# The value's causal convolution as products with diagonal tap matrices

## The reference, cut to what matters

```python
def _short_conv(x, w):
    K = w.shape[-1]                                  # 4
    xp = jnp.pad(x, ((0, 0), (K - 1, 0), (0, 0)))
    y = jnp.zeros_like(x)
    for k in range(K):
        y = y + xp[:, k:k + L, :] * w[:, k]
    return y
...
q = x @ Wq.T;  k = x @ Wk.T;  v = x @ Wv.T
beta = sigmoid(x @ Wb.T)
q = silu(_short_conv(q, conv_q)); k = silu(_short_conv(k, conv_k)); v = silu(_short_conv(v, conv_v))
q = l2norm(q);  k = l2norm(k)                        # per head of 16 channels
# delta rule, per head and token: v_new = (v - k S) * beta;  S += k v_new;  o = q S
```

## Time and profile before

| what | us |
|---|---|
| median of 3 runs (lowest to highest) | 3052.33 (3044.51 to 3056.43) |
| the profiled execution's own time | 3045.67 |
| its span, first to last instruction | 3043.5 |
| VectorE busy in the span | 2124.9 (70%) |
| TensorE products busy in the span | 2498.7 (82%) |
| TensorE weight loads busy | 1887.2 (62%) |
| ScalarE busy in the span | 1605.3 (53%) |
| mean granted TensorE clock | 0.875 |

### The profile page before, as it was taken

How to read it: one execution, slowest core, us unless ns; L and a number is a source line. 1 busy time by engine, 2 the same in 40 slices (tenths; PEclk the granted TensorE clock), 3 DMA queues, 4 the chain that set the end, 5 groups by cost and what they waited for, 6 DMA issues and landing times. The chain is left out here.

```text
span 3043.5 us, 109358 instructions
## 1 busy us (share of the span) xinstructions
PE 2498.7 (82%) x45968; PEld 1887.2 (62%) x45968; DVE 2124.9 (70%) x5160; ACT 1605.3 (53%) x2896; POOL 1112.7 (37%) x1092
## 2 busy tenths in 40 slices
PE   4578887788888878788778999999978898987665
PEld 2345555556565555555566888888867676765443
DVE  4878988899889999888835222222325676878996
ACT  5454555555465554455124555555546666665442
POOL 0000233333333333233433777777744333332000
PEclk8778888888888898788679999999999899999877
DMA  2000122122222122113235999998798575754431
GB/s 66 8 11 10 49 74 71 53 79 75 71 74 73 55 79 73 63 69 111 84 114 172 301 310 305 306 305 296 258 336 305 202 275 209 268 217 173 161 107 28
DMA packets 191579, 448.61 MB, mean 147 GB/s; under 512 B 34034, under 2 KB 83700, under 8 KB 182772
## 3 DMA queue, kind: packets, MB, share of 16 engines
q1 hardware_dynamic: 129652, 284.26, 28.5%
q0 software_dynamic: 52224, 148.97, 12.9%
q10 hardware_dynamic: 9216, 8.39, 0.9%
HBM read 266.07 MB, written 175.42 MB: 145 GB/s over the span
## 5 line engine op out<-in xcount | busy, mean ns | idle before, releaser
L1041 POOL DMA_INDIRECT scr_xs<-xn_r,idx x512 | 534.1, 1043 | 1136.8 <-PE ps L473 479.7
L1068 POOL DMA_INDIRECT scr_ys<-y,idx_t x576 | 578.4, 1004 | 548.0 <-ACT sg L1333 253.1
L712 PE MATMUL ps<-xT,wr 128*128 128x256 f32 (+1 forms) x2560 | 563.5, 364 | 4.7 <-DVE h L2053 4.7
L2053 DVE TENSOR_TENSOR h<-sg,ps 128x256 f32<-128x256 f32 x320 | 125.2, 393 | 532.8 <-ACT sg L1333 532.2
L712 PEld LDWEIGHTS ps<-xT,wr 128*128 128x128 f32 x2560 | 439.1, 193 | 56.1 <-issue 14.1
L720 PE MATMUL ps<-wr,h 128*128 128x256 f32 x1152 | 312.3, 390 | 56.4 <-ACT y L1340 56.3
L1340 ACT ACTIVATE y<-ps,of_row 128x256 f32<-128x256 f32 x576 | 244.8, 471 | 145.2 <-PE ps L720 139.8
L720 PEld LDWEIGHTS ps<-wr,h 128*128 128x128 f32 x1152 | 218.5, 195 | 89.3 <-issue 62.1
L1680 DVE TENSOR_TENSOR tu<-tu,tmp 128x60 f32<-128x60 f32 (+14 forms) x480 | 242.5, 505 | 16.5
L527 PE MATMUL ps<-sq,w_proj 128*128 128x512 f32 x512 | 249.7, 624 | 5.1 <-issue 2.4
L1677 DVE TENSOR_TENSOR tmp<-tu 128x60 f32<-128x60 f32 (+14 forms) x480 | 241.6, 503 | 13.4
(11 more groups left out here) (268 smaller groups left out, 4231.6 us busy)
## 6 DMA issues: line engine op xcount, KB each, us to landing
wr<-in_wexp SPq DMA_DIRECT2D x224, 384.0 KB, 4.5
xt<-scr_xs SPq DMA_DIRECT2D x256, 280.0 KB, 4.2
yg<-scr_ys SPq DMA_DIRECT2D x64, 1024.0 KB, 7.4
scr_ys<-y,idx_t POOLq DMA_INDIRECT x576
scr_xs<-zeros SPq DMA_DIRECT2D x64, 140.0 KB
xt<-scr_xs SPq DMA_DIRECT2D x64, 140.0 KB
x_in<-in_x SPq DMA_DIRECT2D x64, 128.0 KB, 3.1
x_res<-in_x SPq DMA_DIRECT2D x64, 128.0 KB, 2.6
```

The source lines that it names most:

```text
L712: last = pe.matmul(ps[:, bank, half * TILE:half * TILE + wide], wr[:, w % NW, at:at + EI], xT2[:, t % NH, k, 0:wide], start=k == 0, stop=k ...
L1041: nc.gpsimd.indirect_dma_start(xs[int(i >= FIRST)][:, :], bass.IndirectOffsetOnAxis(idx[:, i % NR, c, k:k + 1], 0), xn_r[:, i % NR, c, :], ...
L1068: nc.gpsimd.indirect_dma_start(ys[int(t >= NTH[0])][:, :], bass.IndirectOffsetOnAxis(idx_t[:, t % NRT, r:r + 1], 0), y2[:, t % NY, r, :], ...
```

## The change: what it does, and the diff

The value tiles (4 and 5) are convolved on TensorE. At the start VectorE multiplies the identity by each tap's column and so makes eight diagonal 128x128 matrices. `value_taps` accumulates four products in a PSUM bank, one a tap, with the shifted `raw` as the moving operand; `value_silus` takes the silu straight from that bank. ScalarE no longer makes the scaled copy of the value tiles, and VectorE no longer runs their taps. Queries and keys stay as they were. Two small constants are placed and loaded later, to make room. A new semaphore, `s_values`, tells VectorE that the values are there; `s_silu` and `s_conv` count four tiles a block where they counted six.

```diff
...
+        v_taps = sb1("v_taps", [P, G, KC, P])
...
+            def value_taps(i, g):
+                n = 2 * G + g
+                bank = into(f"TAP{n}", i)
+                ring.emptied(pe, f"PROJ{n}", i)
+                for k in range(KC):
+                    last = pe.matmul(ps[:, bank, :].rearrange("p (b t) -> p b t", b=B), v_taps[:, g, k, :],
+                                     raw[:, n, :, k:k + TB], start=k == 0, stop=k == KC - 1)
+                done(last, bank)
...
                 if A:
+                    value_taps(a, 1)
                     project(a, 7)
                     project(a, 4)
...
                 if A:
+                    value_taps(a, 0)
                     norms(a, 0)
...
-                    nc.scalar.activation(conv[:, n, :].rearrange("p (b c t) -> p b c t", b=B, c=NC), by_chunk,
-                                         ACT.Copy, scale=conv_w[:, n // G, n % G, HIST:])
+                    if n < 2 * G:
+                        nc.scalar.activation(conv[:, n, :].rearrange("p (b c t) -> p b c t", b=B, c=NC), by_chunk,
+                                             ACT.Copy, scale=conv_w[:, n // G, n % G, HIST:])
...
+            def value_silus(i, g):
+                n = 2 * G + g
+                bank = ring.filled(act, f"TAP{n}", i)
+                if i:
+                    act.wait_ge(s_bv, i)
+                last = nc.scalar.activation(conv[:, n, :], ps[:, bank, :], ACT.Silu)
+                last.then_inc(s_xe[bank], 1)
+                ring.emptied(act, f"TAP{n}", i)
+                act.sem_inc(s_values, 1)
...
                 if A:
+                    value_silus(a, 1)
                     betas(a, 1)
...
                     silus(a, 2)
                     silus(a, 3)
+                    value_silus(a, 0)
                     raised(a, 0)
                     raised(a, 1)
-                    silus(a, 4)
                     raised(a, 3)
                     raised(a, 2)
                     norm_logs(a)
...
                     norm_roots(a)
-                    silus(a, 5)
...
             sI.did(V.memset(caps[:], float(CAP)))
+            for g in range(G):
+                for k in range(KC):
+                    sI.did(V.tensor_scalar(v_taps[:, g, k, :], identity[:], conv_w[:, 2, g, k:k + 1], None, ALU.mult))
             sI.wait(dve)
...
             def new_inputs(i):
-                dve.wait_ge(s_silu, 6 * (i + 1))
+                dve.wait_ge(s_values, 2 * (i + 1))
...
                     gated(p, 1)
-                if A:
-                    taps(a, 4, 5)
                 if C:
```

More of the change, by code:

```diff
@@ L168, in network_kernel @@
         identity = sb("identity", [P, P])
-        w_quant = sb("w_quant", [P, G, D])
         one_col = sb("one_col", [P, 1])
@@ L207, in network_kernel @@
         zeros = sb("zeros", [P, 2 * ROW])
-        bias_row = sb("bias_row", [1, 2 * D])
         ones_mean = sb("ones_mean", [P, 2 * NS])
@@ L310, in network_kernel @@
         quantT = sb("quantT", [P, G, N])
+        w_quant = sb("w_quant", [P, G, D])
+        bias_row = sb("bias_row", [1, 2 * D])
         qa0, qb0, qc0 = xq[:].rearrange("p c d -> p (c d)")[:, 0:G * D], qb[:, 0:G * D], qc[:, 0:G * D]
@@ L338, in network_kernel @@
         s_silu = sem("s_silu")
+        s_values = sem("s_values")
         s_sq = sem("s_sq")
@@ L394, in network_kernel @@
                      (w_o[:], wo), (w_gate[:], wgate), (gbias_row[:], gbrow), (lower_tri[:], lower),
-                     (w_shared[:], wshared), (bias_row[:, 0:D], brow[0:1, :]),
-                     (bias_row[:, D:2 * D], brow[0:1, :]),
+                     (w_shared[:], wshared),
                      (ones_mean[:], mean), (b_delta[:], bdelta))
@@ L400, in network_kernel @@
                            for b in range(B))
+        later += tuple((bias_row[:, m * D:(m + 1) * D], brow[0:1, :]) for m in range(2))
         ALL_CONST = 16 * len(constants)
@@ L1101, in _ @@
         def _(act):
-            CONV_ORDER = (2, 3, 0, 1, 4, 5)
+            CONV_ORDER = (2, 3, 0, 1)
             def root(ph, i):
@@ L1191, in silus @@
                 for n in ns:
-                    act.wait_ge(s_conv, 6 * i + CONV_ORDER.index(n) + 1)
+                    act.wait_ge(s_conv, 4 * i + CONV_ORDER.index(n) + 1)
                     nc.scalar.activation(conv[:, n, :], conv[:, n, :], ACT.Silu).then_inc(s_silu, 1)
-                    if n < 2 * G:
-                        act.wait_ge(s_silu, 6 * i + n + 1)
-                        nc.scalar.activation(sq[:, n, :], conv[:, n, :], ACT.Square).then_inc(s_sq, 1)
+                    act.wait_ge(s_silu, 4 * i + n + 1)
+                    nc.scalar.activation(sq[:, n, :], conv[:, n, :], ACT.Square).then_inc(s_sq, 1)
+            def value_silus(i, g):
[7 more added lines that the diff above has]
+                act.sem_inc(s_values, 1)
             def raised(i, *ns):
@@ L1624, in key_rows @@
             def key_rows(i):
-                dve.wait_ge(s_silu, 6 * i + 4)
+                dve.wait_ge(s_silu, 4 * (i + 1))
                 V.tensor_tensor(conv[:, G:2 * G, :], conv[:, G:2 * G, :], sq[:, G:2 * G, :], ALU.mult)\
```

## The result

| | before, us | after, us |
|---|---|---|
| median of 8 runs each (lowest to highest) | 3051.72 (3044.51 to 3056.43) | 3062.79 (3051.71 to 3066.89) |
| profiled execution, span | 3045.67, 3043.5 | 3053.07, 3050.9 |
| mean granted TensorE clock | 0.875 | 0.896 |

The ratio is 1.0037 [1.0022, 1.0053]: slower by some 11 us of the medians, where 25 had been forecast. The sign is clear of the measurement, but the size lies inside the 0.5% that the prediction took as the least that a measurement can tell from no change. Where the text behind this line gives a ratio, it is to the kernel before in the same group of runs.

The account below looks back on a forecast made before the run. Two chains end almost together at the query product: VectorE's, and TensorE's norms with ScalarE's roots. Thirteen blocks +15, first three +9, matrices +1.3: +25 us on 3052.33, so 3077 us; range 3025 to 3125.

Parts of the forecast that it names:

- 40 or more: Sign of being right: VectorE's idle time before the query product grows from 20.2 us to this, released by ScalarE's roots.
- the walk of the block: One block followed on three engines: query product +0.5 us later at full rate, +2.3 with half rate on the taps.
- the forecast of -0.9: Block at 1053 us, where L511 has only a short stall: roots at 1136.5, query product 0.9 us earlier.
- +2.8 forecast: Block at 1143 us, where line 567 already runs at full rate: roots at 1231.6 against 1228.80.
- The sum over thirteen: Blocks with all stages, of three kinds (seven, four and two): 14.4 - 5.8 + 6.1 = +15 us.
- the term of the first three passes: Cold TensorE, taps ahead of the norms: +4, +2 and +3 us, together +9.
- the matrices: Eight tap matrices made by VectorE at the start, before the ready signal: about 1.3 us, counted as +1.3.
- the first rival: TensorE's clock and instruction fetch recover with the added taps: 3035 us, 20% chance.
- Clock and fetch recover: Rival: long taps fill the gap and give the fetch time; seven blocks also lose L511's 2.2 us standstill; 3035 us, 20%.
- Full rate, nothing gained: Rival: full rate but the same stalls, so VectorE time is only traded for a wait; 3053 us, no change, 25%.
- The clearly slower case: Rival: norms become the bound, TensorE as slow as now from line 567 to L1215; +67 us, 3120 us, 15%.
- the first place is free and the second is not: Tile 5's taps ahead of projections 7 and 4 lie in a wait; nothing covers tile 4's 3.70 us before the norms.

Follow-up runs that it names:

- after_fourth: The changed kernel unaltered, run again in the fourth group beside its two halves: 3058.42 us, 1.0054 of the kernel before.
- start_only: The change made in the first three passes alone, the other thirteen as in the kernel before: 3043.54 us, 1.0009.
- rest_only: The change made in the thirteen passes from the fourth on, the first three as in the kernel before: 3057.54 us, 1.0057.
- late4: Changed kernel with tile 4's taps moved behind the norms: 3268.31 us (1.0134), 3261.51 (1.0128) and 3259.06 (1.0119).
- the single tiles: One tile on TensorE, the other left on VectorE: tile 5 alone 3242.52 us (1.0057) and 3242.79 (1.0077), tile 4 alone 3232.78 (1.0051).
- the doubled groups: Changed kernel with one group of taps done twice: tile 5's 3293.1 us (1.0251), tile 4's 3297.63 us (1.0275).
- no_taps: Kernel before without the value tiles' three older taps, nothing added to TensorE: 3200.96 us (0.9973) and 3213.94 us (0.9981).

## Why the prediction was right and wrong

**Right: the direction, and why VectorE's time is not gained.** The prediction put the loss of VectorE's 4.06 us a pass into waits. They are there (59 us in the thirteen passes). The query product's wait for the roots went from 20.2 to 49.4 us, in 16 passes of 16, the "40 or more" that was named. Only 18.9 of the 29 lie in the thirteen passes, though; in the first pass alone it is 12.8 to 21.1, and without that one the sum would be 28.3. And the prediction had made the roots the whole of it: the state (22.4) and the right side (12.2) took nearly twice as much. One reading was off as well: the 75.3 us of standstill in L511 add the idle time of the weight loads to that of the products. In TensorE's own list of waits the products have 24.0 us of it, in 20 times. No term of the sum used it.

**Right: the walk of the block.** Forecast for the query product +0.5 at full rate, +2.3 with half rate on the taps; measured +1.1, with 5.40 us of taps between the 3.70 and the 5.55 of the two cases. By its taps alone the block was nearly the half-rate case; it came out lower because L513 ended 0.7 us earlier against the block's start where 0.2 later had been forecast, and that is luck. Line 567's wait went over to projection 4, and from_state runs 1.31 us with no standstill, both as written. In the block that answers to the earlier trace rows the forecast of -0.9 failed: its L513 stands still for 2.28 us (before 0.38), the taps take 5.05, and the query product starts 88.8 us after the block's start instead of 84.4, +4.4. In the one that answers to the earlier trace rows it failed the other way: +2.8 forecast, 85.4 after the start instead of 85.5 measured, -0.2. The standstills fall elsewhere in each kernel, so a single block is not a forecast. The sum over thirteen came out at +11.3 for +15, out of single passes from -3.7 to +5.1: such a sum comes near in part by luck, and another profile of the changed kernel (after_fourth, in another group of runs) has 1227.5 us for them, 7 more.

**Wrong: the term of the first three passes.** "In the first three blocks ... it is cold, and the taps again stand ahead of the norms", together +9 and +1.3 for the matrices. Up to the start of the thirteen passes the profile has +1.2 us, and not +10.3. The matrices took 1.62 us, as thought, and put the first product on TensorE 1.33 later (17.46 to 18.79). The first block's query product came 4.2 us later (60.9 to 65.0); with the matrices in it, that is +2.8 for the block where +4 had been forecast. One cost in it had been put at nothing: the silu of tile 5 "needs no table load (the gate before it uses the same table)", but in the first three passes no gate stands before it, and the trace has a table load of 1.28 us ahead of it in each. The wait for ScalarE's silu of a value tile (L1216), named as a possible omission, is there with 1.88 us ahead of the second pair of norms. It costs 0.5 at most: the squares that these norms need anyway end at 56.35, and the norms start at 56.89.

The second and third blocks are what failed: +2 and +3 forecast, measured -1.9 and -2.4 (from query product to query product 72.0 to 70.2, and 86.7 to 84.2). For the second the prediction had the bounds, -3.1 with full rate "lets the saved VectorE time show", and took a value nearer the cold end. For the third the measured value lies below even its lower bound of -0.5. Up to the third query product the whole start costs -0.2 us; the rest of the +1.2 comes behind it, where the new state waits 1.25 us for TensorE (L501). The rows show the other end: the taps keep TensorE going ahead of the norms, the norms run at full rate, and the stretch's granted clock rises from 0.76 to 0.82. In the third block a standstill moved too: before the change TensorE stood still for 2.40 us in L511 ahead of the norms, after it for 0.36 in L513 ahead of the taps. start_only confirms the size: 1.0009 [0.9992, 1.0026] where +10.3 us would be 1.0034, outside it. That the clock is the cause is read from the rows and from the two windows of start_only and rest_only; no run held the clock and moved the taps.

The Trainium skill ("TensorE: Matmul & The Clock Gate", What's actually happening) has the slow clock as the default that activity lifts. This trace agrees: 0.76 to 0.82 and 0.86 to 0.90 with more products in the same time. The prediction named this rule on the side of the first rival and gave that rival 20%; it came true in part, in the clock, without making the kernel faster.

With the term of the start at the measured 1.2 instead of 10.3, the sum is 15 + 1 = +16, or 0.5%, inside the interval of the result [0.22%, 0.53%] at its upper end. The rest is the thirteen passes' 15 for 11.3, and the 4.8 us between executions in the last two. Both profiled executions lie below the medians, the one before by 6.0 us and the one after by 9.7, so the medians have +11.1 where the profiles have +7.4.

**The rivals.** "Clock and fetch recover" (3035): the clock did, the fetch did not. Its own words, "the standstill in L511 comes ahead of the second group", hold. The Trainium skill ("Runtime: NRT & Kernel Launch", Instruction fetch mechanics) has the fetch hidden behind the issue; both traces show the small products' standstills, 85.7 and 94.1 us in the four rows above, and the long taps among them have not made them fewer. No run shows that they are a fetch. "Full rate, nothing gained" (3053) was nearer than the forecast: 3062.79 lies between it and 3077. The clearly slower case (3120) did not come; line 567 did not stay cold after its shorter gap.

**The reason behind the forecast held less than its direction.** It said that the first place is free and the second is not. In the runs that could tell (all in the slower groups), both places cost alike, and moving the second behind the norms gave nothing back. So the sum of the thirteen passes was near for a reason that these runs do not bear out. What stands is more general: time added to TensorE is paid for in either place, in those groups 0.4 us for each of the 118 us of the change and 0.7 to 0.8 for each beyond them.

**What stays open.** Whether late4, the single tiles, the doubled groups and no_taps would give the same numbers in the conditions of the result is open: the whole change costs 0.37 and 0.54% there and 1.25% in the slower groups. What the standstills are is open too, and what a microsecond added to TensorE costs in the kernel before. No kernel run here beats the one before; the only one faster, no_taps, leaves work out.

## What to carry to other kernels

Before moving work from the busier engine to the other, read both engines' lists of waits, not their busy shares. If the busier one waits for hardly anything, and the other's longest wait is for it, their chains may end together. Time taken from the busier one then comes back as waits (here 59 us of waits for 48 us saved), while time given to it is paid nearly in full (63 of 65 us), and time given to the other in part (0.4 us each for the first 118, 0.7 to 0.8 behind them). A half-rate stretch is no fixed price of the instructions that now stand in it: work put ahead of them takes it over, so bound it from both sides and let neither end win by habit. And check what a change costs at the start of a program by making it there alone.

## What the runs showed of the hardware

The same program takes different times in different groups of runs: the kernel before 3040.31 us (median of 22) and 3051.72 in two of them, 3219.93, 3217.57, 3208.43 and 3218.76 in four others, each steady within 1%. The five groups of experiments ran on four chips: the second and third on the same one, the first, fourth and fifth each on another; the fourth's chip gave the short time and the other three the long one. The profiles show three differences. In the experts' part the transfers are slower; the stretch 2000 to 2500 of the kernel before in the result's runs and in the first group's (last columns: busy share of the DMA engines and GB/s):

```profile
2000.00:2500.00 500.00, 454.76 (x2593) 383.37 (x2592) 226.32 (x638) 288.06 (x633) 275.78 (x275) 0.96 0.81 279
```

```profile
2000.00:2500.00 500.00, 422.20 (x2142) 359.69 (x2144) 129.16 (x462) 223.97 (x546) 285.36 (x294) 0.94 0.78 258
```

In the same part TensorE stands still ahead of the experts' first products (L712), where the code has it wait for the expert's weights: 98.5 us in 58 times in the first group's profile, with no releaser shown, and no such row in the result's profile of before.

And TensorE stands still more often inside the small products: adding up the rows without a releaser of lines 457, 473, 487, 499 and 511 in its list of waits, 101 times and 110 us in the result's profile of before, 210 times and 142 us in the first group's. Line 487 alone goes from 3 times and 1.5 us to 49 times and 23.3 us. In the result's profile most of these gaps stand 126 to 128 recorded products apart, or a small multiple of that; many of the added ones in the other stand a few products apart.

The passes up to the seventh take about as long in both (it starts at 777.6 and at 779.6 us). Of the 174 us by which the span is longer, 17 arise in the thirteen passes, 25 in the last two, and 132 in the second half of the program. What makes the one time or the other was not tested. It matters for reading this case: in the slower groups the change costs two to three times as much, so an experiment and the result that it is to explain belong among the same runs.
